# Rolling part of a feed-forward group loop, and taking a tile's statistics one step later

## The reference

```python
x = x + 0.5 * ffn(layernorm(x))
x = x + attn(layernorm(x))
x = x + 0.5 * ffn(layernorm(x))

def ffn(x):
    routing   = softmax(x @ gate_w.T)            # 8 experts
    in_scale  = routing @ in_channel_scale       # (tokens, 1024)
    out_scale = routing @ out_channel_scale
    return x * in_scale @ sign(weight).T * out_scale + bias

def attn(x):                                     # width 256, 16 heads of 64, blocks of 128 tokens
    q, k, v = split(conv1d(x, conv_w, 3 taps) + conv_b, 3)
    o = causal_softmax_attention(q @ wq + bq, k @ wk + bk, v @ wv + bv)
    return (o @ wo + bo) @ proj_w + proj_b
```

## Time and profile before

| | |
|---|---|
| median of 3 runs | 1066.08 us (1064.38 to 1067.06) |
| the profiled execution | 1067.06 us, span 1064.9 us |
| PE busy | 935.9 us, 88% of the span |
| DVE busy | 712.6 us, 67% |
| ACT busy | 453.2 us, 43% |
| POOL busy | 370.0 us, 35% |
| first feed-forward, 41 to 245 us | PE busy 175.0 of 204.0 us, DVE 139.2 |
| second feed-forward, 909 to 1060 us | PE busy 147.2 of 151.0 us, DVE 88.1 |

### The profile page before, as it was taken

The page is one execution under the profiler, slowest core; times in us unless marked ns, Lnnn a source line. Parts: engine busy times, 40 slices in busy tenths (PEclk is TensorE's granted clock), DMA queues, the critical chain, the costliest instruction groups (busy, mean ns, idle before and its releaser), DMA issues.

```text
span 1064.9 us, 15007 instructions
## 1 busy us (share of the span) xinstructions
PE 935.9 (88%) x4960; PEld 709.0 (67%) x4960; DVE 712.6 (67%) x1469; ACT 453.2 (43%) x1127; POOL 370.0 (35%) x307
## 2 busy tenths in 40 slices
PE   4788988887989999897978997899798888999997
PEld 2576766663334787786766886777577666778786
DVE  5677776566998888354586388268729947666652
ACT  3434444441224325234665356246435544334331
POOL 2145555573452220000221233214204442455555
PEclk9899999997999999898988998999899999999999
DMA  9333322312333431844002022211141264343233
GB/s 296 129 119 119 121 88 90 138 59 100 99 109 118 161 126 48 328 158 158 2 17 83 1 80 70 70 39 59 59 130 60 83 257 176 131 146 139 91 132 115
DMA packets 41474, 119.95 MB, mean 113 GB/s; under 512 B 5696, under 2 KB 14912, under 8 KB 40000
## 3 DMA queue, kind: packets, MB, share of 16 engines
q1 hardware_dynamic: 41408, 119.11, 32.3%
HBM read 87.64 MB, written 31.46 MB: 112 GB/s over the span
## 4 chain that ended last, share of the span: by engine, by line
PE 52%; DVE 15%; issue 4%; ACT 3%; DMA 1%; SPq 0%; POOL 0%; POOLq 0%; DVEq 0%; ACTq 0%
PE a_p_g L1763 18%; PE a_p_g L620 11%; PE c_p_m L1217 5%; PE c_p_m L1219 3%; PE c_p_m L1220 3%; PE c_p_m L1221 3%; PE a_p_s L1787 3%; DVE c_xs_lo L1625 2%; PE a_p_t L1797 2%; PE a_p_o L1811 2%; DVE a_s L1660 2%; DVE a_sums L1663 2%; PE a_p_s L563 1%; DMA c_raw<-in_conv_w_dram 1%; ACT a_s L1559 1%
## 5 line engine op out<-in xcount | busy, mean ns | idle before, releaser
L1492 POOL TENSOR_TENSOR a_s<-a_s,a_sums 128x512 f32<-128x512 f32 x64 | 66.5, 1040 | 304.3 <-DVE a_sums L1669 304.3
L272 POOL TENSOR_TENSOR f_y<-f_y,f_res 128x512 f32<-128x512 f32 x64 | 82.8, 1293 | 144.2 <-DVE f_y L474 143.6
L1559 ACT ACTIVATE a_s<-a_s,a_nmx 128x128 f32<-128x128 f32 x256 | 99.4, 390 | 49.0 <-DVE a_nmx L1665 49.0
L1763 PE MATMUL a_p_g<-c_xs_hi,x_room 128*128 128x512 f32 x256 | 101.9, 446 | 13.5 <-DVE c_xs_lo L1625 7.4
L620 PE MATMUL f_p_m<-f_wsign,f_a_hi 128*128 128x512 f32 x256 | 105.3, 411 | 0.0
L620 PE MATMUL a_p_g<-f_wsign,f_a_hi 128*128 128x512 f32 x256 | 103.4, 404 | 0.0
L620 PE MATMUL f_p_m<-f_wsign,f_a_lo 128*128 128x512 f32 x256 | 101.5, 397 | 0.0
L620 PE MATMUL a_p_g<-f_wsign,f_a_lo 128*128 128x512 f32 x256 | 101.1, 395 | 0.0
L1217 PE MATMUL c_p_m<-c_vf,c_ring_f 128*128 128x512 f32 x192 | 86.6, 608 | 10.2 <-DVE c_ring_f L894 7.1
L269 POOL TENSOR_TENSOR f_res<-f_res,f_hbias 128x512 f32<-128x512 f32 x64 | 83.7, 1307 | 11.3 <-DMA f_res<-x_after_attention 7.3
L1219 PE MATMUL c_p_m<-c_vh,c_ring 128*128 128x512 f32 x192 | 77.3, 402 | 8.6 <-DVE c_ring L1100 6.9
(11 more groups left out here) (218 smaller groups left out, 2216.9 us busy)
## 6 DMA issues: line engine op xcount, KB each, us to landing
c_raw<-in_conv_w_dram SPq DMA_DIRECT2D x24, 768.0 KB, 4.3
f_w_raw<-in_w_t_dram SPq DMA_DIRECT2D x8, 1024.0 KB, 10.6
f_res<-in_x_dram SPq DMA_DIRECT2D x16, 512.0 KB, 4.3
x_after_ffn<-f_y SPq DMA_DIRECT2D x8, 1024.0 KB, 6.3
f_xin<-x_after_attention SPq DMA_DIRECT2D x8, 1024.0 KB, 5.5
f_res<-x_after_attention SPq DMA_DIRECT2D x16, 512.0 KB, 4.2
out_dram<-f_y SPq DMA_DIRECT2D x8, 1024.0 KB, 6.3
f_xin<-in_x_dram SPq DMA_DIRECT2D x7, 1024.0 KB, 5.3
```

The lines of the kernel that those rows point to most:

```text
L272: pool.tensor_tensor(y[:, p, t, h], y[:, p, t, h], res[:, t, h], ALU.add).then_inc(y_done, 1)
L1492: pool.tensor_tensor(s[:, r], s[:, r], sums[:, r].unsqueeze(2).broadcast_to([P, 4, P]), ALU.mult).then_inc(probs_ready, 1)
L1559: done = act.activation(s[:, r, h, :], s[:, r, h, :], ACT.Exp, bias=nmx[:, r, h:h + 1], scale=SCALE, accum_out=sums[:, r, h:h + 1])
L1763: mm = pe.matmul(p_g[:, bank, :], a, b, start=n == 0, stop=n == len(pairs) - 1)
```

## The change

`group_loop` writes out group 0, runs groups 1 to 4 as two passes of a loop on the chip whose body holds an odd and an even group, and writes out groups 5, 6 and 7. In the looped groups g is a register, so the semaphore values and some addresses are computed by register instructions. Looped bodies can't leave out a step at an edge, and all that a looped group looks ahead to must exist: x is therefore loaded three groups ahead instead of four, and its statistics are taken at the start of the group that normalises it instead of at the end of the one before. Both hold for all groups, looped or not.

```diff
 def group_loop(eng, body):
-    for g in range(NG):
+    body(0, 0)
+    with eng.Fori(0, (NG - 4) // 2) as i:
+        body(2 * i + 1, 1)
+        body(2 * i + 2, 0)
+    for g in range(NG - 3, NG):
         body(g, g % 2)
...
         def load_x(g, p):
-            if isinstance(g, int) and g in (2, 3):
-                sp.wait_ge(t_full, 4 * g - 4)
+            if isinstance(g, int) and g == 2:
+                sp.wait_ge(t_full, 4)
...
-            if exists(g + 4):
-                sp.wait_ge(t_full, 4 * g + 12)
-                load_x(g + 4, p)
+            if exists(g + 3):
+                sp.wait_ge(t_full, 4 * g + 8)
+                load_x(g + 3, 1 - p)
             if exists(g - 1):
                 for t in range(FT):
                     sp.wait_ge(y_done, 4 * g - 2 + 2 * t)
...
         def body(g, p):
             for q in range(4):
+                if q == 0 and exists(g + 3):
+                    stats(g + 3, 1 - p)
                 if q == 0 and X is not None and exists(g - 1):
                     out_stats(g - 1, 1 - p)
...
                 if q == 3 and exists(g + 1):
                     low(g + 1, 1 - p, KD - 1)
-                if q == 3 and exists(g + 4):
-                    stats(g + 4, p)
```

More of the change, by code:

```diff
@@ L711, in _ @@
                     f.load_res(0, t)
-                f.load_x(3, 1)
                 group_loop(sp, f.body)
@@ L748, in _ @@
                 f.softmax(1)
-                f.stats(3, 1)
                 group_loop(dve, f.body)
@@ L1456, in _ @@
                 s2.load_res(0, t)
-            s2.load_x(3, 1)
             for t in range(GT):
@@ L1719, in _ @@
             s2.softmax(1)
-            s2.stats(3, 1)
             group_loop(dve, s2.body)
```

## The result

The changed kernel takes 1074.95 us (median of 4 runs, 1073.34 to 1075.46), the kernel before 1065.32 (1064.38 to 1067.06, 4 runs). The ratio is 1.0086, with a 95% interval from 1.0067 to 1.0104: 7 to 11 us slower, where I had forecast 3.65 and a range that ended a little over 1073.3. The profiled execution of the changed kernel took 1072.67 us, its span is 1070.8 us, against 1064.9 before. That is less than any of its four timed ones, and the 1067.06 profiled before was the most of four, so the two profiles hold less of a difference (5.6 us) than the medians do (9.6).

The account below looks back on a forecast made before the run. PE was taken as busiest, held up in the first feed-forward by ACT and DVE. Terms 2.95 - 0.7 + 1.4 = +3.65 us gave 1069.7 us from the median 1066.08; range 1064.3 to a little over 1073.3.

Parts of the forecast that it names:

- Part 1: First feed-forward: 2.9 us of statistics move behind the multiplication into y; +0.95 us at three borders, -0.45 at the first.
- +0.95 us: First feed-forward, three later borders: the output's statistics on DVE start later by this, and PE stalls by the same amount.
- The first border's -0.45: First feed-forward, first border: the multiplication could have started much earlier, so the move gains 0.45 us.
- the 2.9 us taken from the twin: DVE, first feed-forward: length of the moved statistics, taken from the output's statistics, 2.9 us.
- Part 2: Group borders: residual loads no longer queue behind the x load, so GpSimd's first add starts earlier and collides with DVE's normalise.
- +0.6 us at two borders: Borders before groups 2 and 3, first feed-forward: GpSimd's earlier add collides with normalise, +0.6 us each.
- The -0.65: First feed-forward, group 2: slow small DVE op at 103.00, hit by the late add, goes; PE saves 0.65 us.
- x itself lands a few us later: x load issued one body later; costed at nothing, since a whole group's work hides it.
- Part 3: Second feed-forward: moving the statistics is free by some 0.5 us; residual in time gives -0.7 us.
- The -0.7: Second feed-forward: saving from PE's 0.48 us idle at 958.17 and a tie before it; bounds 0 and -0.7.
- Part 4: The loop itself: register waits at ACT's hand-overs cost +1.4 us together; jump and registers cost PE nothing while work is queued.
- the 0.08 per hand-over: ACT, looped groups: each hand-over whose last wait is a register instruction's costs 0.08 us.

Follow-up runs that it names:

- c_residual_first: Kernel before with only the residual loads and store of a body put ahead of its x load; 1068.23 us against 1064.98.
- k_both_undone: a_written_out with GpSimd's differences one body later and second feed-forward's x group 3 loaded ahead of attention's stores; 1068.88 us against 1064.63 before.
- j_x3_late: Kernel before with second feed-forward's x group 3 load moved behind attention's last four stores; 1066.12 us against 1064.63.
- a_written_out: Changed kernel with all eight groups written out, no loop; 1072.33 us against 1064.98 for the kernel before.
- l_before_again: The kernel before, unchanged, for a second profile; 1059.97 us (1 run) against 1064.63.
- e_no_differences: Kernel of b with GpSimd's two differences per group left out; 1070.18 us (1 run) against 1065.61 for the kernel before.
- h_differences_moved: Kernel of b with GpSimd's differences done one body later, where GpSimd idles; 1071.47 us against 1065.61 for the kernel before.
- f: c_residual_first with the statistics put into DVE's idle time at q = 3 in both feed-forwards; 1066.02 us against 1065.61 for the kernel before.
- g: Changed kernel with second feed-forward's x group 3 load put back ahead of attention's last four stores; 1071.97 us against 1065.61 for the kernel before.
- b: Kernel before with only the statistics moved to the start of the body, loads unmoved, nothing looped; 1072.43 us against 1064.98.
- d_one_pass_loop: Kernel before, order untouched, with groups 1 and 2 of both feed-forwards as a loop of one pass; 1067.14 us against 1064.98.
- i: Kernel of f with the statistics in DVE's gap in the first feed-forward only; 1063.09 us against 1064.63 for the kernel before.

## Why the prediction was wrong

- **Part 1, the move past the multiplication: the failed step.** "+0.95 us" for each of three borders holds for the part that I worked out: c_residual_first's 25.70 became 26.60 in k_both_undone, +0.90. The first border's -0.45 was -0.52 (28.06 to 27.54). (The 142.42 in it takes 0.44 us for a matmul whose row says 0.40, a slip of 0.04.) What failed is the step before it, the 2.9 us taken from the twin: that is the statistics' length where nothing disturbs them. In the new place their last op meets `differences`, and in the written-out kernel they take 4.0 us at each of three borders: 27.63 to 27.67 against 26.60, +1.05 each. I had asked what GpSimd's first add does to DVE, and not what GpSimd runs under the statistics. In the changed kernel itself f_vpe took 0.33, 1.21 and 1.32 us at these borders, which fits its shorter group 2. PE's waits there, which I had put at some 1.4 us each, came to 1.1, 2.0 and 2.1 us, spread over two scales.
- **Part 2, the residual.** The +0.6 us at two borders was right, and GpSimd no longer waits for `f_res`, as forecast. The -0.65 was too small and not sure to be there: the slow op costs 1.0 us of group 2 and shows in three of four profiles. "x itself lands a few us later ... I cost that at nothing" holds inside the loop and fails at the second feed-forward's first group, where "later" means behind attention's stores: this second failed step, a term put at nothing, is +1.6 us in the changed kernel, and 2.8 to 3.1 in j_x3_late and a_written_out together with a spell of low clock. That term had been in front of me: the diff takes `s2.load_x(3, 1)` from ahead of the stores.
- **Part 3.** Inside the looped groups the move was free, as worked out. The -0.7 was one execution's: l_before_again has neither the stall at 958.17 nor the 19.05 of group 0. Its place is real but its size is chance. Of the seven profiles with the old order of the loads, three lose more than 0.5 us in one group to a late residual that brings GpSimd's work over the softmax (21.33 before, 21.86 in e_no_differences, 24.30 in h_differences_moved, against 20.62); of the seven in which no x load holds the residual up, none does.
- **Part 4, the loop.** I charged 1.4 us; 0.3 us shows in the groups, and the times can't tell 0.3 from 1.4. PE's wait for ACT's X was 8.5 and is 8.3, so the 0.08 per hand-over seen on ACT did not reach PE there.
- **Sum.** With the measured sizes: 5.2 (first feed-forward) + 1.6 (late x) + 0.3 (loop) = 7.1 us, the lower end of the measured interval. The remaining 2.5 us are not traced to a cause. They are less than what unchanged stretches differ by from one profile to the next, and whether the loop has a share in them is open. Part of them may be the low clock behind the stall of 2.14 us (1.7 us). It is not the change's own: it is there in after, e, f, g, h and j and absent in both profiles of before, a, b, c, d, i and k. With it the stretch took 79.7 to 79.9 us, without it 78.1 to 78.3, and h (81.2) and k (79.7) have the moved differences' cost on top.

The Trainium skill, "SBUF — State Buffer", in its section on the two sides of the memory, says that an op of DVE in a two-port mode, or one with two inputs there, and GpSimd's op exclude each other for a whole instruction. The trace agrees with the exclusion: the small op waited 1.15 us for a subtraction of 1.28, while the output's statistics, one input each, ran beside the same subtractions in 2.47 us. The small op has one input too; by that rule it would have been in a two-port mode, which no trace here shows.

## What to carry to other kernels

When work is moved along one engine, lay it over the timeline of the engine that shares the memory with it, at its new time, and look at its smallest ops: they lose a whole op of the other. When a load is moved into a loop body, look at what stands ahead of it on its queue at the loop's first pass. Before a slow op of a profile is booked as a saving, see it in more than one other execution: one without it does not show that it was an accident.

## What was not expected of the hardware

- An op of 0.17 us took 1.21 to 1.32 us beside GpSimd's subtraction; the statistics op was not slowed at all. The collision is a matter of tenths: 0.33, 1.21 and 1.32 us in one execution.
- A PE stall of about 2 us was followed by some 3 us at the lower clock, 1.2 GHz, in six of the fourteen profiles and not in the other eight, with stalls of 2.04 to 2.14 us in both: 2.14 in after and before (the windows above). That nearly doubled the price of the stall, by 1.7 us behind one of 2.14.
- The register instructions of a looped group showed as 0.07 us in a group of 20.7 in the second feed-forward; in d_one_pass_loop, whose loop runs once, the looped groups took 20.62 us as in the kernel before.
